# A two-layer transformer block on one NeuronCore: the dense feed-forward moved behind the expert sum and the last attention, its products gathered in the expert sum's PSUM bank

## The reference

```python
# layer 0
xn = layernorm(x)
x  = x + channel_attention(xn) + mixture(xn)     # 64 experts of 88, top 8, and 2 shared
# layer 1
xn = layernorm(x)
x  = x + window_attention(xn) + dense(xn)        # window 64, top 32 of it, 8 heads
# dense: the feed-forward that is moved
h = xn @ (ternary(w_fc) * scale).T + gate * (xn @ v.T @ fast_b.T @ u.T)
r = maximum(h, 0.0)
dense = (r * r) @ (ternary(w_proj) * scale).T    # 128 -> 512 -> 128
```

## Time and profile before

| | us |
|---|---|
| median of 3 runs | 772.04 (766.23, 772.04, 772.14) |
| profiled execution, its time | 761.87 |
| profiled execution, span of the trace | 760.1 |
| mean granted TensorE clock | 0.948 |

### The profile page before, as it was taken

The page is one execution under the profiler, slowest core; times in us unless marked ns, Lnnn a source line. Parts: engine busy times, 40 slices in busy tenths (PEclk is TensorE's granted clock), DMA queues, the critical chain, the costliest instruction groups (busy, mean ns, idle before and its releaser), DMA issues.

```text
span 760.1 us, 11266 instructions
## 1 busy us (share of the span) xinstructions
PE 690.4 (91%) x3208; PEld 468.9 (62%) x3208; DVE 608.9 (80%) x2520; ACT 424.2 (56%) x763; POOL 423.1 (56%) x515
## 2 busy tenths in 40 slices
PE   2999999999999899999999899999999999788533
PEld 2656765666656577776555676766566677566433
DVE  3898697659979889989769897975858999759973
ACT  4654543657557665564866665456758564377200
POOL 2165456454656775685628677565745666613540
PEclk9989999999999999999999999999999999997555
DMA  9930000000000000001000000001000000010000
GB/s 285 362 80 1 2 0 0 2 1 16 17 1 5 6 13 18 11 4 34 14 1 6 10 8 15 14 5 31 17 1 2 19 11 13 13 40 11 20 26 17
DMA packets 25722, 21.90 MB, mean 29 GB/s; under 512 B 1920, under 2 KB 23596, under 8 KB 25148
## 3 DMA queue, kind: packets, MB, share of 16 engines
q1 hardware_dynamic: 25660, 21.18, 9.4%
HBM read 18.95 MB, written 2.23 MB: 28 GB/s over the span
## 4 chain that ended last, share of the span: by engine, by line
PE 60%; DVE 21%; ACT 6%; DMA 4%; issue 4%; POOL 3%; SPq 1%; DVEq 0%; POOLq 0%; ACTq 0%
PE bank_X L507 19%; PE bank_U L507 14%; PE bank_A L507 13%; PE bank_G L507 13%; DVE S L797 4%; DVE Wk L1214 4%; DMA vw<-vscratch 4%; DVE m L1211 3%; SPq L409 1%; ACT L1285 1%; PE bank_X L767 1%; DVE Wlo L797 1%; ACT L1280 1%; PE bank_X L516 1%; POOL S L1523 1%
## 5 line engine op out<-in xcount | busy, mean ns | idle before, releaser
L507 PE MATMUL bank_A<-S,WdT 128*128 128x512 f32 x368 | 183.2, 602 | 3.1 <-DVE S L797 1.9
L1523 POOL TENSOR_TENSOR Wlo<-Wgu,Whi 128x256 fp32r<-128x256 f32 x138 | 109.3, 797 | 120.8 <-ACT Whi L1280 120.0
L797 DVE TENSOR_TENSOR S<-S,bank_U 128x512 f32<-128x512 f32 x184 | 123.7, 680 | 52.2 <-PE bank_U L507 30.7
L1280 ACT ACTIVATE S<-bank_G 128x512 f32<-128x512 f32 x184 | 107.8, 595 | 95.4 <-PE bank_G L507 89.0
L1523 POOL TENSOR_TENSOR S<-S,Rb 128x512 f32<-128x512 f32 x88 | 119.1, 1355 | 50.2 <-DVE S L797 49.8
L1280 ACT ACTIVATE Whi<-Wgu 128x256 fp32r<-128x256 f32 x184 | 74.2, 413 | 70.8 <-PE bank_U L507 62.2
L507 PE MATMUL bank_G<-xH,Whi 128*128 128x512 f32 x184 | 93.2, 506 | 2.4 <-ACT S L1280 1.2
L507 PE MATMUL bank_U<-xH,Whi 128*128 128x512 f32 x184 | 91.6, 498 | 3.5 <-DVE S L797 3.5
L507 PEld LDWEIGHTS bank_A<-S,WdT 128*128 128x128 f32 x368 | 66.0, 191 | 45.0 <-issue 26.8
L1214 DVE MATCH_REPLACE8 Wk<-m,Wk 128x79 f32<-128x79 f32 x384 | 82.0, 225 | 0.0
L797 DVE TENSOR_TENSOR S<-S,Rb 128x512 f32<-128x512 f32 x88 | 77.4, 881 | 1.8
(11 more groups left out here) (235 smaller groups left out, 1312.6 us busy)
## 6 DMA issues: line engine op xcount, KB each, us to landing
vw<-vscratch SPq DMA_DIRECT2D x32, 158.0 KB
Wgu<-in_Wgu SPq DMA_DIRECT2D x2, 2048.0 KB, 15.4
xs<-in_x SPq DMA_DIRECT2D x4, 256.0 KB, 7.0
wqk<-in_w_qkv SPq DMA_DIRECT2D x1, 1024.0 KB, 7.6
Wgu<-in_Wgu SPq DMA_DIRECT2D x1, 1024.0 KB, 9.4
vscratch<-mo SPq DMA_DIRECT2D x4, 256.0 KB
out<-xs SPq DMA_DIRECT2D x3, 256.0 KB, 2.3
Wgu<-in_Wgu SPq DMA_DIRECT2D x1, 512.0 KB, 5.4
```

The source lines that it names most:

```text
L507: return engine.matmul(dst, lhsT, rhs, start=start, stop=stop)
L797: return engine.tensor_tensor(dst, a, b, op)
L1280: return engine.activation(dst, src, f, bias=bias, scale=scale, accum_out=acc)
L1523: return engine.tensor_tensor(dst, a, b, op)
```

## The change

Four things change.

- `uses()`: ff1 of all batches stands behind the last attention in bank `X0`. ff2 moves to bank `A`, one use per batch; a tile has 128 of its columns, so all four tiles of a batch fill the bank.
- TensorE's first ff2 step of a batch waits for `mo` of batch 3 (`pe.wait_ge("mo", B)`), since bank `A` is the expert sum's until then. ScalarE's Relu waits for ff2 of two tiles earlier by a new semaphore, `ff2_tile`, since `PR` is no longer guarded by the bank.
- VectorE adds a batch's 128x512 at once: 4 steps in place of 16.
- `yT` of a batch must live longer: two tiles `yT0`, `yT1` for batches 0 and 1, and `xTs[0]`, `xTs[1]` for 2 and 3.

All order strings are new. In the SP string the stores of batches 0 to 2 now stand among the value loads of batch 3: the last 16 letters read st_v3, s0, g0, g1, s1, g2, g3, s2, g4, g5, s3.0, s3.1, g6, g7, s3.2, s3.3; before they read, with s2 behind st_v3, g0 to g4, s3.0, g5, s3.1, g6, g7, s3.2, s3.3. The TensorE string has 21 letters f ahead of the last e before, and one after.

```diff
--- before.py
+++ after.py
@@ -37,38 +37,38 @@
 ORDER = {
     "sp":
-        "vvvvvvvvvsvvvvvvvvvsvvvvvvvvvvsvvvvvsvsvvss",
+        "vvvvvvvvvvvvvvvvvvvvvvvvvvvvsvvsvvsvvssvvss",
     "pe":
...
-        "aeheeaeeheeahmehmeameemhmheeeeehmmmemeeehaeeeemmmeheeaedeeedeeedemmdedmeeemmtmeadteedeeeetemtmmmdmee"
-        "eaemmeeteteetfmmemeetmfeteeeeeememfmfteeeetefteemtetmeefmmmmtmmhtfttfthfhthfhhfhhfffhhfddddfdddttttd"
-        "tttttttttttttttt",
+        "hheeehheammmmmeehmheeeedededeemmmdmeedmaeadtateeeememeeetemtmmdadmeefeemtteeeemeteeeemeetmmteeemmeme"
+        "eeemtemeteeeetemmmeeteetemmeeeemmteeemmmtmtmhfftftffhfhthfhfhhffhffhhffddffffdffddtfftdftftddffttftf"
+        "ttfffttttttttttt",
     "dve":
...
-        "okkkoeekkkkkkkkeomelkeegkkkmkkmgekaeemlkemgkeakkkemlgkkkeemekekfgklekefmmgekekgkklegmkkemekkkgfhkhhh"
-        "gfhhghogfhhfhhfhhokkkokfkkkkkkkkkgokgkkkkkkkkggkkkkgkkkgkkkgkkkgkkkkgkkgggg",
+        "emeegmkkkkaekelmagkkkkgeelmekemkelgkkeemgkkkeemeklgememeklgkkeemkkemgekelmekemgkekkgkkhhhhghhghofhhh"
+        "hhhokfkkkkkkkokkkkkkogkkfgkkkgkkgkkkkgkkkkfgkkgkkgkkkkkgkkkgggg",
...
@@ -167,7 +167,7 @@
     def dense(b):
         for i in range(NT):
             add("X0", "ff1", b, i)
-            add("X0", "ff2", b, i)
+        add("A", "ff2", b)
 
     for n in range(B * NF):
         add(f"G{n % 2}", "g", n)
@@ -189,10 +189,9 @@
         if b + 1 < B:
             add("X0", "sp", b + 1, 0)
             add("X0", "sp", b + 1, 1)
-            dense(b - 1)
             add("X0", "sp", b + 1, 2)
-    dense(B - 2)
-    dense(B - 1)
+    for b in range(B):
+        dense(b)
     for b in range(B):
         last = b == B - 1
         for what in ("mo", "y", "enc", "met", "nm"):
@@ -308,7 +307,7 @@
         ln1 = sb("ln1", [128, 6, NT])
         yn = mo[:, :].rearrange("p (a c) -> p a c", a=NT)
         vt = yn
-        yT = sb("yT", [128, T])
+        yTs = [sb(f"yT{i}", [128, T]) for i in range(2)]
         kp = sb("kp", [128, PADK + T])
         ksq = sb("ksq", [128, T])
         mk2 = sb("mk2", [128, PADK + T])
@@ -398,7 +397,7 @@
             return (B - 1) * (NG // 2) + g + 1
 
         def yT_of(b):
-            return xTs[0] if b == B - 2 else yT
+            return yTs[b] if b < 2 else xTs[b % 2]
 
 
 
@@ -479,7 +478,7 @@
             def store(b, i, n):
                 j = i + n - 1
                 sp.wait_ge(empty(bank("dec", b, j)), nth("dec", b, j) + 1)
-                sp.wait_ge(empty(bank("ff2", b, j)), nth("ff2", b, j) + 1)
+                sp.wait_ge(empty(bank("ff2", b)), nth("ff2", b) + 1)
                 load("st_out", out[b].rearrange("(i p) c -> p i c", p=128)[:, i:i + n, :],
                      xs[:, NT * b + i:NT * b + i + n, :])
 
@@ -662,12 +661,14 @@
                                yTb[:, 128 * i:128 * i + 128])
                     p.then_inc(sems(full(bank("ff1", b, i))), 1)
                     yield
-                    t = fill("ff2", b, i)
+                    if i == 0:
+                        t2 = fill("ff2", b)
+                        pe.wait_ge("mo", B)
                     pe.wait_ge("ffsq", b * NT + i + 1)
                     r = PR[:, 512 * (i % 2):512 * (i % 2) + 512]
                     for k in range(4):
-                        p = mm(t[:, 0:128], r[:, 128 * k:128 * k + 128], WpT[:, k, :], k == 0, k == 3)
-                    p.then_inc(sems(full(bank("ff2", b, i))), 1)
+                        p = mm(t2[:, 128 * i:128 * i + 128], r[:, 128 * k:128 * k + 128], WpT[:, k, :], k == 0, k == 3)
+                    p.then_inc(sems("ff2_tile"), 1)
 
             def routes():
                 for b in range(B):
@@ -1099,19 +1100,18 @@
                 stt(mb[:, 2:3], mb[:, 0:1], 0.1, mb[:, 1:2], ALU.mult, ALU.add).then_inc(sems("mb"), 1)
 
             def dense(b):
-                x = xb(b)
-                for i in range(NT):
-                    yield
-                    t = filled("ff2", b, i)
-                    after_adds(b)
-                    latest[b] = emptied(tt(x[:, i, :], x[:, i, :], t[:, 0:128], ALU.add), "ff2", b, i)
+                x = xb(b).rearrange("p a c -> p (a c)")
+                yield
+                dve.wait_ge("ff2_tile", NT * (b + 1))
+                after_adds(b)
+                latest[b] = emptied(tt(x, x, ps("ff2", b)[:, :], ALU.add), "ff2", b)
 
             def head(b):
                 x = xb(b)
                 xf = x.rearrange("p a c -> p (a c)")
                 yield
                 t = filled("mo", b)
-                dve.wait_ge(*latest[b])
+                dve.wait_ge(empty(bank("att", b)), nth("att", b) + 1)
                 a = emptied(tt(xf, xf, t[:, :], ALU.add), "mo", b)
                 yield
                 dve.wait_ge(*a)
@@ -1413,6 +1413,8 @@
                     r = PR[:, 512 * (i % 2):512 * (i % 2) + 512]
                     yield
                     t = filled("ff1", b, i)
+                    if b * NT + i >= 2:
+                        sc_.wait_ge("ff2_tile", b * NT + i - 1)
                     a = emptied(act(r, t[:, :], ACT.Relu), "ff1", b, i)
                     sc_.wait_ge(*a)
                     act(r, r, ACT.Square).then_inc(sems("ffsq"), 1)
@@ -1425,12 +1427,8 @@
                 act(ln1[:, 2:3, :], ln1[:, 2:3, :], ACT.Exp, scale=-0.5).then_inc(sems("s_rs"), 1)
                 yield
                 t = filled("y", b)
-                if b == B - 2:
+                if b >= 2:
                     sc_.wait_ge(full(bank("att", b)), nth("att", b) + 1)
-                elif b > 0:
-                    p = b - 1 if b < B - 2 else b - 2
-                    sc_.wait_ge(full(bank("ff1", p, NT - 1)), nth("ff1", p, NT - 1) + 1)
-                    sc_.wait_ge(full(bank("v", p)), nth("v", p) + 1)
                 emptied(act(yTb[:, :], t[:, :], ACT.Copy), "y", b)
                 yield
                 t = filled("enc", b)
```

More of the change, by code:

```diff
@@ L46 @@
-        "mhmemeeheemmeeeeeehhmheeememhmeeeeeymmmeeeehaemheaedeedemaedeaedadeaatdtmmmmemdteemeemdteeememeemaee"
-        "etameeetaeametmmeeeemtseetsefmmfemeeeeefmmemteetmeetemfmfmtfteeeeeefeeefmmteeehestmtmseatmtmameeeamt"
-        "aeheeaeeheeahmehmeameemhmheeeeehmmmemeeehaeeeemmmeheeaedeeedeeedemmdedmeeemmtmeadteedeeeetemtmmmdmee"
-        "eaemmeeteteetfmmemeetmfeteeeeeememfmfteeeetefteemtetmeefmmmmtmmhtfttfthfhthfhhfhhfffhhfddddfdddttttd"
-        "tttttttttttttttt",
-    "dve":
[L52 to L57, removed]
-        "okkkoeekkkkkkkkeomelkeegkkkmkkmgekaeemlkemgkeakkkemlgkkkeemekekfgklekefmmgekekgkklegmkkemekkkgfhkhhh"
-        "gfhhghogfhhfhhfhhokkkokfkkkkkkkkkgokgkkkkkkkkggkkkkgkkkgkkkgkkkgkkkkgkkgggg",
@@ L60 @@
-    "act":
[L61 to L66, removed]
+        "yyeeeyeemeeeameeeeaeeeaeayeasessasammmmmeeeeemeememmeeeumemeeeememaueeemameeeeueeemueyaymeeeeyammmem"
@@ new lines @@
+        "emeeeememeeeememeeemmemeemeeyeemmmseseeeeemeeeeemmmeemsmeeeeseemmeemeeeeyeeyeeemmyhmmemeeemeeemeeeme"
+        "meemhmheheehheehmhmeememeehmheeeemededeedyeemedmmdmmaetdeaeteaeeeaemaeemeamdtammedteeeemmeemmeeeeeem"
+        "teteetemtmemmteeameeaeeeaemtmateeteemeestmmeseestemeemsmeemmeeeemtyeehmmeetyeemmeeeteemeetemtehyhmee"
+        "mmteehmeeheehmmhemeeehmemeemeeemeyeeeeemmaeeeheaheaedadadadadtdmmmteeeeedtmemmtmmedateeeemmeeateetme"
+        "emateeeemtaeeeemmmeemmtemtseeeemtsmseeeestmmeeeeetmeeemeeaemtemeeaethatmeeeemmeatheteameeehmmetemeha"
@@ new lines @@
+        "hheeehheammmmmeehmheeeedededeemmmdmeedmaeadtateeeememeeetemtmmdadmeefeemtteeeemeteeeemeetmmteeemmeme"
+        "eeemtemeteeeetemmmeeteetemmeeeemmteeemmmtmtmhfftftffhfhthfhfhhffhffhhffddffffdffddtfftdftftddffttftf"
+        "ttfffttttttttttt",
+    "dve":
+        "yyyyyycyyecyyyyelyyyyyyyeeyyyayelyyayeyyecyyyaylammaymyeemaeemeaueemulemauueuueuumeeluueemmleemayyyl"
+        "aeyyemeyyyyyyemeyleymyyeyyyemeyyyemelemyyyyeemleemeylyemeemeelmeeeemylyhyehehmheyyemlyyeyeyyymhhyyyy"
+        "eelhoemheyhmeyhyhhlemyeeehymyelmoekkykokkkeakkeeaolmmgeekkkkakkkamlkeakeegmemaekkelmaekemgekkglkkaem"
+        "gekkeemkkkalkgeemkemgakekeymelykyemkkkygeelyekkemeghlehehhmkemgeelhhymgeeyyyyegmyhyyeylyymeyoeyhmhyy"
+        "yeyylyeymyehemeyemhlehemaeahloakkkaakkkokkkkkkaeogekmkeamkkgkalkeemkegkemekekgklmkekkakeegmelmkeakge"
+        "mekkklemkegkemekkkemlgekeekkleagemeamhghhhelhheemgaemegeholmhaehahhemheeahlmeeoamekkaokkkkkklkemeokk"
+        "emeegmkkkkaekelmagkkkkgeelmekemkelgkkeemgkkkeemeklgememeklgkkeemkkemgekelmekemgkekkgkkhhhhghhghofhhh"
+        "hhhokfkkkkkkkokkkkkkogkkfgkkkgkkgkkkkgkkkkfgkkgkkgkkkkkgkkkgggg",
@@ new lines @@
+    "act":
+        "yxxxyyexecxexexeexcexxaayxssxsyaseeeexexexxeexaxeexxeuaexxaeexxuxeuxyeyxexeexexexexeexxexexexeyxexse"
+        "xexsxexeyxexeesxeexxexseexxyxeyxxmeeexxexeexxeheexhhhxexhexhhxeeehxkkexxexnkeknnxnkyxxnknkenegekxeae"
+        "xxaexexnnangexexxeexxeexexgnxeaxngeexeaxeaxxeegxexexsegsxesxyxexeesxemxexeyxegexxexexhyxgeehxhexehxe"
+        "xehxeexxheexexxyeehxxeexxhxkkanaxknknnkannknkgkeenexxngeanxeeaxxeenexgxnaexexexgexxeexexgsexexsseexx"
```

(6 more changed lines are left out.)

## The result

| | before | after |
|---|---|---|
| median, us | 769.65 (4 runs, 766.23 to 772.14) | 744.25 (4 runs, 741.67 to 748.00) |
| span of the profiled execution | 760.1 | 739.9 |
| last expert sum copied at (ACT, `mo<-bank_A`) | 653.09 | 630.22 |
| group 2's value load of batch 3 issued | 698.66 | 678.10 |

The ratio is 0.968, 95% interval 0.961 to 0.974. I had forecast 757.5 us, a factor of 0.981 and a range of 747 to 772: the direction held, the size did not. The kernel gained 25.4 us by the medians, 20.2 by the spans.

A forecast was written before the change was run, and what follows sets the result against it. TensorE's work was taken to bound the kernel up to the last expert sum, serial value loads the tail. Terms -18.0 + 2.9 + 0.8 = -14.3 us of span, factor 0.981, gave 757.5 us; range 747 to 772.

The forecast's parts named there:

- the first term: TensorE ahead of the last expert sum: 20 dense steps go, at 0.89 us each, taken as -18.0 us.
- the lower end: Same stretch: local peaks of VectorE's choose steps eat part of the gain, leaving half, 9 us.
- The way to ctx(3, 0), +2.9: From last expert product to ctx(3, 0): VectorE +1.7, ScalarE +1.2, TensorE steps +1.0, clock -1.0; together +2.9 us.
- The first, +1.7: VectorE ahead of the addition of `mo`: one more choose step and a mask, +1.7 us.
- The second: ScalarE in head(3): pair relu1.1 between the metric's exponential and logarithm delays VectorE's metric chain, +1.2 us.
- The credit for the clock: At ctx(3, 0) and the turn ahead: more work keeps TensorE's clock until then, -1.0 us, between 0 and -1.3.
- SP's queue, +0.8: Among batch 3's value loads: store 2's 256 KB share the engines, +0.8 us; waits of stores 0 and 1 cost 0.
- The end as ctx(3, 0) plus 61.4: Tail: value loads run one after another, so the end is ctx(3, 0) plus 61.4 us.
- B: Rival: VectorE leads in the choose stretches, stream ends 9 us earlier, not 18; -5.3, 766.7 us, chance 0.20.
- C: Rival: `X0` chain freed, stream gives 21.6, no loss before ctx(3, 0); -20, 751.7 us, chance 0.13.
- A: Rival: TensorE's clock falls to its lower level behind the stream; +6.5 in all, 778.6 us, chance 0.15.
- The base: Whole kernel: the factor 0.981 was put on the median of 772.04; the profiled execution (761.87) was 1.3% faster.

The follow-up runs named there:

- the move alone: Changed kernel with the order strings of before, only letters f placed behind their new neighbours and SP's string new: 789.75 us, ratio 1.035.
- the 80-row runs: Value loads of 80 rows in place of 79: on the changed kernel 733.73 us, ratio 0.957; on the kernel before 754.24 us, ratio 0.985.

## Why the prediction was wrong, step by step

The forecast of 757.5 us was 13.3 us too high. 6.0 of them lie in the sum (-14.3 us of span forecast, -20.2 measured), 7.3 in the base on which its factor was put.

**The step that failed is the first term: 20 steps off TensorE, -18.0 us.** Measured by the last expert product it was -22.4 (646.46 to 624.10). The term was short by 4.4 us and, worse, had the wrong reason. I took "TensorE is busy 98%, so what leaves it leaves the time". In the old order that is false: the move alone gave 0.3 us of the stretch, the removal of all dense work 4.9. In the new order it holds: 18.6 us put back cost 17.5. What I had called the lower end, that local peaks of VectorE's choosing eat the gain, is what the move alone does, and to the full, not to a half; that the choosing is what stood in the way is shown for the old order without dense work, where relieving it gave 15.0 us. What I had no term for is that the new strings themselves take out TensorE's waits. Of the stretch's 28.8 us (494.4 to 465.6) 21.9 are busy time and 6.9 are waits, 9.8 before and 2.9 after. Of the 28.8 again 5.9 are only shifted, since the first copy comes 5.9 us later; that leaves the 22.9 by which the last sum comes earlier. The busy time fell by more than the 21 steps are worth because 24 of the other matmuls went from the stretch to the front of batch 0's sum.

**How much each part gives** can only be said in an order. Move first: 0, then the strings, everything. Strings first, with products of about the same busy time still in the stream (but none of the dense steps' waits): 494.4 - 483.1 = 11.3 us of the stretch, of which some 5.9 are shifted, so about 5; then taking them out, 17.5. With nothing dense anywhere the strings gave 17.7. What the strings would give with the real dense steps and their waits in the stream is open: no run had them in the new order. Open is also whether a new search for the old placement would have found some of the gain.

**The way to ctx(3, 0), +2.9.** It measured +2.3 from the last sum (45.6 to 47.9) and +1.8 from the last expert product (52.2 to 54.0), so the sum nearly held, but two of its parts did not, and that is luck. The first, +1.7 for VectorE's steps ahead of the addition of `mo`, measured +0.3: the last product at 626.98 us is followed by the addition at 632.80, 5.8 us against 5.5, with three choose steps and a mask between them and not four. The second did not hold as told: swapping the pair of ScalarE gained nothing. TensorE's own string puts nm3, the product that `Pk` copies, behind ff2(1, 1) and ff1(1, 2), which need the same pair: TensorE waits 2.02 us for its Square, and 2.11 with the swap. So the pair is in the way on TensorE whichever stands first on ScalarE. The credit for the clock held: ctx(3, 0) took 1.06 us after, 2.08 before.

**SP's queue, +0.8.** Measured +0.4 to the last landing (53.93 against 53.57). With -22.4 and +1.8 that makes the -20.2 us of span. The stores' waits at 0: shown by the run with all stores last.

**The end as ctx(3, 0) plus 61.4.** It held, 61.8. Only the loads' nature was left as a cited rule; the 80-row runs agree with it.

**The rivals.** B, only half comes out: not here, though its mechanism is real and decides in the old order. C, 751.7 us: its span, 760.1 - 20 = 740.1, is what came, and it is the nearest, but `X0`'s chain was not its reason, since taking the dense steps out of `X0` in the old order gave 4.9 us of the stretch. Its terms were also added wrongly: -21.6 and +0.8 are -20.8, which would be 750.9 us. A, the clock: the opposite came behind the stream. The dense steps hold the clock up to ctx(3, 0), and without them it falls.

**The base.** The larger piece of the miss is the scale. The spans give a factor of 739.9 / 760.1 = 0.973; on my base of 772.04 that would have been 751.5 us, inside the range. The other 7.3 us lie in the base. The profiled execution before (761.87) stands 1.3% under the median that I multiplied, the one after (741.67) only 0.3% under its own. The old kernel's executions went from 760.7 to 773.7 us, those of the changed one from 741.7 to 748.0, and with the old kernel the mean granted clock goes along: 0.941 to 0.954 in those up to 766.7 us, 0.932 to 0.939 in those from 771.1 on, while the changed kernel has 0.951 to 0.955 in all its executions. So the old kernel has less clock in some executions and the changed one does not. Where it loses it isn't shown, since the profile before is of an execution with 0.948.

## What to carry to other kernels

An engine that is 98% busy sets the pace only if nothing else is nearly as late at the places where it waits; before pricing work taken off it, ask which engine would lead next, stretch by stretch, and whether the written order was fitted to the old balance. A move and the order searched for it are one change: the move alone gave nothing here. In a tail where TensorE idles, work moved there can be free or better, since here it held the clock; and a load's partition count is worth a look before its bytes.

## What I had not expected of the hardware

- Removing 256 matmuls and their ScalarE and VectorE work from the kernel in its new order made it 3.4 us slower (747.63 against 744.27), by the clock behind the stream: 0.63 against 1.00.
- In the changed kernel the granted clock fell to 0.50 inside the stream for a slice of 18.5 us in which TensorE was never idle; from 376 to 386 us, just ahead of the fall, it was not idle either.
- A DMA of 79 partitions x 4 rows of 512 bytes takes 8.6 us of a queue's time, one of 80 partitions lands in 2.3 us with its latency.
- While such a load is under way, SP stands in the issue of the next transfer: 8.26 us for a store of 64 KB, 7.54 for one of 256 KB in the profile after. In the changed kernel with loads of 80 rows its stores take 0.36 to 0.43 us. The timelines of the SP queue show the store of batch 2, first in the changed kernel:

```profile
685.81 7.54 SPq L408 DMA_DIRECT2D out<-xs  x1
```

Then in the changed kernel with loads of 80 rows:

```profile
686.33 0.39 SPq L408 DMA_DIRECT2D out<-xs  x1
```
